# Weighing two chunks of attention together in every second slot, and turning the self stage's next input in the middle of slots 2 and 3

## What is computed

```
ln_out = layernorm(hidden_states, ln1_s, ln1_b)
qkv = ln_out @ w_qkv + b_qkv
...
ctx = merge_heads(attention(split_heads(q), split_heads(k), split_heads(v), ltor_mask))
x = hidden_states + ctx @ w_ao + b_ao
ln_out = layernorm(x, ln2_s, ln2_b)
...
x = x + cross_out
mlp_out = gelu(layernorm(x, ln3_s, ln3_b) @ w1 + b1) @ w2 + b2
return x + mlp_out
```

## Time and profile before

| | us |
|---|---|
| median of 3 runs (1925.21 to 1925.41) | 1925.25 |
| the profiled execution | 1924.46 |
| its span in the trace | 1922.6 |
| TensorE busy with matmuls | 1848.2 (96%) |
| VectorE busy | 987.7 (51%) |
| ScalarE busy | 985.1 (51%) |
| GpSimd busy | 581.5 (30%) |

### The profile page before, as it was taken

The page is one execution under the profiler, slowest core; times in us unless marked ns, Lnnn a source line. Parts: engine busy times, 40 slices in busy tenths (PEclk is TensorE's granted clock), DMA queues, the critical chain, the costliest instruction groups (busy, mean ns, idle before and its releaser), DMA issues. The chain is left out here.

```text
span 1922.6 us, 40249 instructions
## 1 busy us (share of the span) xinstructions
PE 1848.2 (96%) x13328; PEld 1490.5 (78%) x13328; DVE 987.7 (51%) x3402; ACT 985.1 (51%) x3138; POOL 581.5 (30%) x714
## 2 busy tenths in 40 slices
PE   5999999999999999999999996999999999999999
PEld 3787777877876787878878774888888888888887
DVE  4665665756666766766667664523232322323211
ACT  2776666766676767766777674432222222222222
POOL 3443443443444443433434433402020101010110
PEclk9999999999999999999999997999999999999999
DMA  6121111111111321221212224010101010201010
GB/s 201 60 70 49 46 46 49 52 54 46 57 61 48 109 76 53 70 69 57 68 60 63 84 77 147 12 55 12 55 11 55 11 60 5 65 0 65 0 44 22
DMA packets 71103, 108.07 MB, mean 56 GB/s; under 512 B 12544, under 2 KB 20736, under 8 KB 71040
## 3 DMA queue, kind: packets, MB, share of 16 engines
q1 hardware_dynamic: 71040, 107.27, 17.8%
HBM read 82.07 MB, written 25.17 MB: 56 GB/s over the span
## 5 line engine op out<-in xcount | busy, mean ns | idle before, releaser
L939 POOL TENSOR_TENSOR a_p_s<-a_p_s,a_rcp 128x512 f32<-128x512 f32 x256 | 272.9, 1066 | 660.0 <-DVE a_rcp L772 660.0
L660 ACT ACTIVATE a_p_s<-a_t_s,a_mx 128x128 f32<-128x128 f32 x1024 | 398.8, 395 | 4.1 <-DVE a_mx L763 4.1
L1090 PE MATMUL m_ps_h<-mlp_xT,wt 128*128 128x512 f32 x1536 | 377.3, 396 | 1.8 <-PEq L355 1.8
L1104 PE MATMUL m_ps_y<-m_down_hi,m_g_r 128*128 128x512 f32 x1024 | 343.7, 395 | 0.1
L1090 PEld LDWEIGHTS m_ps_h<-mlp_xT,wt 128*128 128x128 f32 x1536 | 288.0, 188 | 71.3 <-issue 2.5
L1182 DVE TENSOR_TENSOR m_g_r<-m_g_t,m_g_r 128x512 fp32r<-128x512 f32 x128 | 95.5, 746 | 473.2 <-ACT m_g_r L1161 473.1
L753 DVE TENSOR_TENSOR a_ps_s<-a_ps_s,a_m_mul 128x512 f32<-128x512 f32 x256 | 176.5, 690 | 114.0 <-PE a_ps_s L467 113.4
L763 DVE CUSTOM_DVE_ANT_0 a_t_s<-a_ps_s,a_m_add 128x128 f32<-128x128 f32 x1024 | 230.9, 281 | 6.2 <-DVE a_ps_s L753 6.1
L1104 PEld LDWEIGHTS m_ps_y<-m_down_hi,m_g_r 128*128 128x128 f32 x1024 | 192.4, 188 | 44.8 <-issue 0.5
L1145 ACT ACTIVATE m_g_t<-m_ps_h,bias_cols 128x512 f32<-128x512 f32 x128 | 88.1, 688 | 269.5 <-PE m_ps_h L1090 269.3
L509 PE MATMUL a_ps_q<-wt,a_cT 128*128 128x512 f32 x768 | 215.1, 416 | 1.8 <-DVE a_cT L784 1.4
(11 more groups left out here) (77 smaller groups left out, 2432.0 us busy)
## 6 DMA issues: line engine op xcount, KB each, us to landing
a_x_t<-in_x SPq DMA_DIRECT2D x32, 256.0 KB, 2.7
a_res_t<-in_x SPq DMA_DIRECT2D x32, 256.0 KB, 2.7
x_after_self<-a_y_t SPq DMA_DIRECT2D x32, 256.0 KB, 2.0
a_x_t<-x_after_self SPq DMA_DIRECT2D x32, 256.0 KB, 2.6
a_enc_t<-in_ctx SPq DMA_DIRECT2D x32, 256.0 KB, 3.3
a_res_t<-x_after_self SPq DMA_DIRECT2D x32, 256.0 KB, 2.7
raw_wt<-in_w SPq DMA_DIRECT2D x32, 256.0 KB, 4.2
x_after_cross<-a_y_t SPq DMA_DIRECT2D x32, 256.0 KB, 2.0
```

The lines of the kernel that those rows point to most:

```text
L660: last = nc.scalar.activation(p_s[:, n % 2, j], t_s[:, n % 2, j], ACT.Exp, scale=-1.0, bias=mx[:, n % 2, j:j + 1], accum_out=sums[:, n % 2 ...
L939: nc.gpsimd.tensor_tensor(p_s[:, n % 2], p_s[:, n % 2], rcp[:, n % 2].unsqueeze(2).to_broadcast([P, HQ, P]), ALU.mult).then_inc(s["normal" ...
L1090: last = nc.tensor.matmul(ps_h[j % 2][:], w1[hw][:, j // KC, kc, (j % KC) * P:(j % KC + 1) * P], xT[:, hx, kc], start=(k == 0), stop=(k == ...
L1104: last = nc.tensor.matmul(ps_y[b][:], g_r[:, j % 2, hg, b * P:(b + 1) * P], w2[hw][:, j // KC, j % KC], start=(j == 0 and x == 0), stop=(j ...
```

## The change

Two edits, in `flips` and in TensorE's `slot`. The line numbers of what follows the second one grow by one.

```
@@ -289,7 +289,7 @@
                     at_end = {(gN - 1, 4): (gN, 0), (gN - 1, 5): (gN, 1), (gN, 0): (gN + 1, 0), (gN, 1): (gN + 1, 1)}
                     return [("x", *at_end[g, n])] if last and (g, n) in at_end else []
                 if not crosses(g + 1):
-                    return [("x", g + 1, n - 2)] if last and n in (2, 3) else []
+                    return [("x", g + 1, n - 2)] if not last and n in (2, 3) else []
                 if opens(g + 1):
                     return [("x", g + 1, n - 2), ("enc", g + 1, n - 2)] if last and n in (2, 3) else []
                 if last:
@@ -605,7 +605,8 @@
                             values(g, n - 1, 0)
                         if n >= 4 and nxt:
                             keys(g + 1, n - 4)
-                        if cur if n >= 3 else prev:
+                        if n % 2 == 0 and (cur if n >= 4 else prev):
+                            weigh_values(*lag(g, n, 4))
                             weigh_values(*lag(g, n, 3))
                         for what, k, b in flips(g, n, nxt, False):
                             (flip_x if what == "x" else flip_enc)(k, b)
```

## The result

The change takes **1890.97 us** (median of four runs, 1887.92 to 1893.62) against 1925.23 before: a ratio of 0.982 with a 95% interval of 0.9807 to 0.9832, 34.3 us less. Measured again later, in five runs, it took 1887.28 us (1886.44 to 1892.57; ratio 0.9809, 0.9796 to 0.9823). The forecast was 1887.4. The profiled execution took 1890.94 us with a span of 1889.1, which is 33.5 less than the span before.

What follows compares the result with a forecast made beforehand. TensorE's own list of work bounds attention (busy 577.87 of 600 us). Savings of 38.4 - 5.0 + 3.0 + 1.5 = 37.9 us from the median 1925.25 give 1887.4 us; range 1873 to 1899, up to 1910 with rivals.

Steps and rivals of the forecast that it cites:

- Merged bursts: Attention's weighing: 256 bursts become 128, a pair costs 0.80 us instead of 1.10, saving 38.4 us.
- One sign: TensorE's timeline after: keys to queries 1.36 us apart in odd slots.
- Rival A: Weighing bursts: second chunk's weight loads wait for the first's matmuls; a pair saves 0.12 us, time 1910; chance 0.08.
- Rival B: Weighing bursts: the 0.55 us belongs to each chunk, not the tile shape change; pairing saves nothing, no change; chance 0.05.
- Cross stage, slot 3: Chunk 1's transposes: TensorE comes 0.55 us earlier, waits 0.31 for GpSimd's normalising; 5.0 us given back over 16 groups.
- Self stage: Turned inputs: waits of 0.24 (slot 3) and 0.38 us (slot 4 keys) go, 0.42 comes; net 3.0 us saved.
- Slot 7: Chunk 5's transposes come 0.32 us late behind GpSimd's normalising, covered by the scores' wait; costs nothing, at most 10 us.
- Start: Before group 0: ScalarE casts the turned input before key weights, keys begin earlier; 1.5 us saved, from none to 2.5.
- 128 x 0.30: Merged bursts' sum over all attention groups: 128 pairs, each 0.30 us less, 38.4 us.
- Rivals C and D: C: other short waits take half, 1903, chance 0.12; D: VectorE's normalisation in slots 6 and 7 slows, 1942, chance 0.04.

Runs made afterwards that it cites:

- experiment 7: The change, but in slots 2 and 6 the pair's first chunk is weighed at the head of the slot, apart from the second: 1907.92 us (0.9910).
- experiment 4: The change, but in the self stage the second turned input's transposes stand at the end of slot 2, not mid slot 3: 1886.40 us (0.9789).
- experiment 2: The kernel before with the self stage's inputs turned earlier alone, each chunk still weighed in its own slot: 1918.88 us (0.9966).

## Why the prediction was right

**Merged bursts: right in mechanism and size.** 0.31 to 0.33 us per pair against 0.30, with 0.64 us for the burst against 0.67. One sign failed: keys to queries is 1.47 us in the odd slot (129.47 - 128.00), not 1.36. So of the 0.55 for a single burst only 0.44 lies between keys and queries (1.91 - 1.47); the rest lies in the queries, which take 1.36 in slot 5 (130.83 - 129.47) and 1.48 behind a single burst (242.74 - 241.26). The price was right and its place was not. Rival A is out: sixteen loads lie within 0.38 us, so the second chunk's do not wait for the first's matmuls, and the rule of the Trainium skill cited there ("TensorE: Matmul & The Clock Gate", part 3) stays contradicted for column tiles. Rival B is out by experiment 7.

**Cross stage, slot 3: right.** From the first turned encoder input (830.58 before, 670.40 after) to the transposes it is 3.95 us instead of 4.20: 0.25 of the 0.55 stays, 0.30 goes back; forecast 0.31. A cross group got 1.11 shorter against 0.89 (1.20 - 0.31): pairs a little cheaper, and a wait of 0.16 before that input, which I had not listed, is gone.

**Self stage: the waits right, the sum a little low.** Gone 0.26 and 0.38, new 0.48 (forecast 0.24, 0.38, 0.42). A self group is 1.59 shorter against 1.40. The second turned input also got cheaper by its place, some 0.06: from the output rows to the transposes it is 122.35 - 119.03 = 3.32 us with one between, and 2.89 without in experiment 4, so it costs 0.43; behind the transposes of slot 3 it cost 0.49 in the trace before (298.64, 299.13 and 299.66 us: transposes, turned input, scores; scores directly behind transposes take 0.53). The first one was not measured apart.

**Slot 7: right.** The transposes wait for GpSimd, the scores' wait covers it; the group pays nothing.

**Start: the right sign; the size hangs on where one reads it.** The first keys come 1.2 us earlier. Group 0's second scores come 2.5 to 4.1 earlier in three profiles (the change's two and experiment 2), but the wait at the keys of slot 4 takes most or part of that back: at group 1's second scores, less what a steady group saves, 0.2 to 1.8 us are left, against 1.5 and a range from none to 2.5. The prediction did not have this wait.

**The step that failed** is 128 x 0.30, at its ends. Twelve of the pairs belong to groups 15, 16 and 31, the first two at the crossing, where TensorE waits for GpSimd in any case: a burst taken out there only joins two waits to one, and in some places the clock falls behind it. The forecast priced the crossing like a steady group, from the mean of one long window. In place of some 3 us less the crossing took 2.7 more in the first profile and about as long as before in the second. Another 1.9 us are lost after the last scores: 0.56 before the first matmul of the MLP and 1.39 behind it, where the granted clock is 0.83 over 10 us and was 1.00. Together this ate the 5 to 6 us that the steady groups gave above forecast and more, so part of the sum's closeness is luck: misses that offset each other.

**Rivals C and D** did not come: no further wait took half, and VectorE's normalisation kept its mix: from 100 to 500 us, 23 of the 48 steps before and 24 of the 50 after took about 1.2 to 1.7 us.

## What to carry to other kernels

Count how often TensorE goes from full-width products to small tiles and back, rather than the small matmuls: joining two bursts saved 0.31 to 0.33 us here, and putting one next to another kind of tile work 0.14 to 0.25. Two edits that act on neighbouring waits must be tried together; here 0.5 us per group came only with both. And where a saving leaves TensorE idle, leave the work in place: behind the joined waits the clock could fall, and keeping the old order there made the crossing 0.9 to 3.6 us shorter.

## What was not expected of the hardware

One wait of 1.93 us cost more than waits of 0.92 and 0.37 us with work between: behind it the granted clock went from its upper level (1.00) to its lower one, and the next work took 1.55 us longer. In the second profile of the change the same wait, 1.92 us, had no fall behind it, only the one of 2.49 us did. In runs of one and the same kernel this happened once or three times in the crossing, which is 2.6 us of the spread. And a burst of tiles of 32 columns starts as long after one of tiles of 32 rows as a full-width product does: 1.10 us from the scores to either. Whether the change from one kind of tile to the other is free is not shown: eight of the scores' steps of 0.126 would be 1.01 us.
